# Attention's score tiles: 4 tokens by 16 heads, two stacked on the partitions, in place of 8 tokens by 16 heads

## What is computed

```python
qkv = qkv.reshape(n, t, 3, H, DH)                 # H = 16, DH = 18
q, k, v = (qkv[:, :, 0], qkv[:, :, 1], qkv[:, :, 2])
attn = jnp.einsum('nthd,ntkd->nthk', q * scale, k)  # 16 x 16 for each token
attn = jax.nn.softmax(attn, axis=-1)
out = jnp.einsum('nthk,ntkd->nthd', attn, v)
```

## Time and profile before

| | |
|---|---|
| median of 3 runs | 426.82 us (426.48 to 428.12) |
| the profiled execution | 426.86 us |
| its span, first instruction to last | 425.1 us |
| PE busy | 402.0 us (95%) |
| PEld busy | 262.3 us (62%) |
| DVE busy | 290.0 us (68%) |
| ACT busy | 232.0 us (55%) |
| granted TensorE clock | full (1.0) in every stretch |

### The profile page before, as it was taken

The page is one execution under the profiler, slowest core; times in us unless marked ns, Lnnn a source line. Parts: engine busy times, 40 slices in busy tenths (PEclk is TensorE's granted clock), DMA queues, the critical chain, the costliest instruction groups (busy, mean ns, idle before and its releaser), DMA issues.

```text
span 425.1 us, 11334 instructions
## 1 busy us (share of the span) xinstructions
PE 402.0 (95%) x4579; PEld 262.3 (62%) x4579; DVE 290.0 (68%) x792; ACT 232.0 (55%) x485; POOL 112.6 (26%) x133
## 2 busy tenths in 40 slices
PE   8999999999989999999977888879999999999996
PEld 4665555666556666666645565657755566666675
DVE  2688885677678846667667866666989776646452
ACT  3356434432266988987786686565776351422100
POOL 5039999950009600000000000004520110101040
PEclk9999999999999999999999999999999999999999
DMA  5999000000000000000000000000000000000011
GB/s 163 303 316 269 24 4 3 11 8 0 2 0 2 2 2 3 2 3 3 2 4 3 5 3 5 2 3 2 2 0 2 14 29 14 15 28 15 29 43 42
DMA packets 7926, 14.68 MB, mean 35 GB/s; under 512 B 2555, under 2 KB 6239, under 8 KB 7748
## 3 DMA queue, kind: packets, MB, share of 16 engines
q1 hardware_dynamic: 7874, 13.96, 11.0%
HBM read 11.52 MB, written 2.38 MB: 33 GB/s over the span
## 4 chain that ended last, share of the span: by engine, by line
PE 74%; DVE 12%; ACT 9%; issue 5%; ACTq 0%; DVEq 0%
PE psum L943 13%; PE psum L959 12%; PE psum L509 9%; PE psum L789 7%; PE psum L773 3%; DVE MX L1356 2%; ACT scratch L1054 2%; PE psum L609 2%; PE psum L866 2%; PE psum L691 2%; PE psum L920 2%; PE psum L621 2%; ACT big L1087 2%; PE psum L737 2%; PE psum L714 2%
## 5 line engine op out<-in xcount | busy, mean ns | idle before, releaser
L943 PE MATMUL psum<-scratch,W 128*128 128x512 f16 (+1 forms) x252 | 57.9, 379 | 0.0
L959 PE MATMUL psum<-W,big 128*128 128x288 f16 x432 | 55.1, 286 | 0.0
L498 POOL TENSOR_TENSOR X<-X,big 128x288 f32<-128x288 f32 x16 | 13.0, 825 | 152.8 <-ACT big L1160 152.5
L1185 ACT ACTIVATE big<-psum 128x512 f32<-128x512 f32 x36 | 21.3, 597 | 57.3 <-PE psum L943 52.3
L959 PEld LDWEIGHTS psum<-W,big 128*128 128x128 f16 x432 | 42.2, 98 | 12.9
L789 PE MATMUL psum<-WQ,scratch 128*128 128x288 f16 (+1 forms) x336 | 49.2, 287 | 1.1 <-DVE scratch L1351 1.1
L1356 DVE TENSOR_REDUCE MX<-psum 128x8 f32<-128x1024 f32 x32 | 39.0, 1220 | 10.9 <-PE psum L737 10.5
L509 PE MATMUL psum<-ident 128*32 128x192 f32 (+3 forms) x142 | 42.7, 385 | 0.0
L1115 ACT ACTIVATE big<-psum 128x1024 f32<-128x1024 f32 x32 | 32.9, 1032 | 14.2 <-PE psum L829 13.9
L943 PEld LDWEIGHTS psum<-scratch,W 128*128 128x128 f16 (+1 forms) x252 | 24.7, 98 | 25.6
L1054 ACT ACTIVATE scratch<-psum,MOD 128x512 f32<-128x512 f32 (+3 forms) x48 | 34.3, 772 | 10.3 <-PE psum L714 6.2
(11 more groups left out here) (218 smaller groups left out, 781.2 us busy)
## 6 DMA issues: line engine op xcount, KB each, us to landing
X<-in_x_dram SPq DMA_DIRECT2D x4, 576.0 KB, 15.1
out_dram<-big SPq DMA_DIRECT2D x16, 144.0 KB, 1.7
big<-in_L_cond_W_dram SPq DMA_DIRECT2D x1, 2268.0 KB
big<-in_L_cond_ada_w_dram SPq DMA_DIRECT2D x2, 864.0 KB, 18.4
stage<-in_L_cond_fc_w_dram SPq DMA_DIRECT2D x1, 1296.0 KB, 19.0
big<-in_L_cond_fc_w_dram SPq DMA_DIRECT2D x1, 1152.0 KB
stage<-in_L_cond_qkv_w_dram SPq DMA_DIRECT2D x1, 864.0 KB
big<-in_L_cond_fc_w_dram SPq DMA_DIRECT2D x3, 144.0 KB
```

The source lines that it names most:

```text
L943: mm = pe.matmul(FB[idx % 3], W1[0:r, w_, P * m:P * m + P], HT[0:r, n % 2, a_, :], start=(p_ == 0), stop=(p_ == 6))
L959: mm = pe.matmul(YB[t % 2][:, 0:D], g[:, a_, f, cols], W2[:, w_, f, :], start=(f == 0 and a_ + w_ == 0), stop=(f == NF - 1 and w_ == 1))
L1185: act.activation(G32[:, idx % 2, :], FB[idx % 3], ACT.Gelu, scale=1.0 / (FINE * FINE)).then_inc(gelu_sb, 1)
```

## The change

A score tile now has 4 tokens x 16 heads = 64 rows and 64 columns, and two such tiles (`e` = 0, 1) stand one above the other on the partitions of the same columns. A unit still fills 128 x 1024 of PSUM, but its 32 tiles hold 128 tokens. So there are 16 units, exponentials and maxima in place of 32, a group is 2 units in place of 4, and AHEAD holds 8 maxima, one in each three slots. The matmuls of a unit are more and smaller. All values_out are ACT's, and v_late's four parts stand in one step. The core of the diff:

```diff
+        pairs = sb("pairs", [P, P])
-        OT = [scratch[:, o + a_ * 5 * CH // 2:o + a_ * 5 * CH // 2 + CH] for a_ in range(2)]
+        OT = scratch[:, o:o + 2 * CH].rearrange("p (a e j) -> p a e j", a=8, e=2)
-        UNITS = 16 * B
+        UNITS = 8 * B
+        HALF = P // 2
-        AHEAD = {24 + 3 * s_ // 2: s_ for s_ in range(16)}
-        LATER = {st: 1 for st in range(16)}
-        ROWS_LATER, ROWS_BANK = {8: 2, 16: 3}, {8: VB[0], 16: MXB[0]}
-        PAIRED = 18
-        DVE_AT = 17
+        AHEAD = {24 + 3 * s_: s_ for s_ in range(8)}
+        LATER = {st: 1 for st in range(8)}
+        ROWS_LATER, ROWS_BANK = {4: 2, 8: 3}, {4: VB[0], 8: MXB[0]}
+        PAIRED = 8
@@ pool: a permutation for the turn after the loop, in place of ident @@
+            for e in range(2):
+                chain(pool.tensor_copy(pairs.rearrange("p (h e m) -> p e h m", h=H, e=2)[:, e],
+                                       ident[:, P // 2 * e:P // 2 * e + P // 2].rearrange("p (h m) -> p h m", h=H)))
@@ maxima (scores has the same loops, with MROWS + 1 rows) @@
-                for g in range(4):
-                    for c_ in range(2):
-                        mm = pe.matmul(MXB[c_][:, P * g:P * g + P], operand(s_, c_, 0, g, MROWS), operand(s_, c_, 1, g, MROWS),
-                                       start=True, stop=True)
+                for g in range(8):
+                    for e in range(2):
+                        for c_ in range(2):
+                            mm = pe.matmul(MXB[c_][HALF * e:HALF * e + HALF, HALF * g:HALF * g + HALF], operand(s_, c_, 0, g, e, MROWS),
+                                           operand(s_, c_, 1, g, e, MROWS), start=True, stop=True)
@@ values @@
-                for c_ in range(2):
-                    if q == 0 and w:
-                        pe.wait_ge(ot_ready, 2 * w + c_ - 1)
-                    for g in range(4):
-                        mm = pe.matmul(PO[c_][32 * g:32 * g + 32, P * q:P * q + P], VG[:, w % 2, c_, 4 * q + g, :],
-                                       E[:, s_ % 2, c_, P * g:P * g + P], start=True, stop=True)
+                    if w:
+                        pe.wait_ge(ot_ready, 2 * w)
+                for q in (2 * q2, 2 * q2 + 1):
+                    for c_ in range(2):
+                        for g in range(4):
+                            for e in range(2):
+                                rows, at, to = slice(HALF * e, HALF * e + HALF), HALF * (4 * (q % 2) + g), HALF * (4 * c_ + q)
+                                mm = pe.matmul(PO[e][32 * g:32 * g + 32, to:to + HALF], VG[rows, w % 2, c_, 4 * q + g, :],
+                                               E[rows, s_ % 2, c_, at:at + HALF], start=True, stop=True)
@@ the loop of PE @@
-                if st % 4 < 2 and 4 <= st // 4 + 1 < UNITS // 4:
-                    for q in range(2 * (st % 4), 2 * (st % 4) + 2):
-                        v_late(st // 4 + 1, q)
-                if st >= 4 and st % 4 == 2:
-                    turn_values(st // 4 - 1)
-                if st % 4 == 3 and st // 4 + 1 < UNITS // 4:
-                    v_groups(st // 4 + 1)
+                if st % 2 == 0 and 4 <= st // 2 + 1 < UNITS // 2:
+                    for q in range(4):
+                        v_late(st // 2 + 1, q)
+                if st >= 2 and st % 2 == 1:
+                    turn_values(st // 2 - 1)
+                if st % 2 == 1 and st // 2 + 1 < UNITS // 2:
+                    v_groups(st // 2 + 1)
@@ the loop of ACT @@
-                if st < DVE_AT:
-                    if st >= 4 and st % 4 == 0:
-                        values_out(st // 4 - 1)
+                if st >= 2 and st % 2 == 0:
+                    values_out(st // 2 - 1)
```

More of the change, by code:

```diff
@@ L826, in scores @@
                     pe.wait_ge(mr_ready, 2)
-                for g in range(4):
-                    for c_ in range(2):
-                        mm = pe.matmul(SB[s_ % 2 if s_ > PAIRED else 0][c_][:, P * g:P * g + P], operand(s_, c_, 1, g, MROWS + 1),
-                                       operand(s_, c_, 0, g, MROWS + 1), start=True, stop=True)
+                for g in range(8):
+                    for e in range(2):
+                        for c_ in range(2):
+                            mm = pe.matmul(SB[s_ % 2 if s_ > PAIRED else 0][c_][HALF * e:HALF * e + HALF, HALF * g:HALF * g + HALF],
+                                           operand(s_, c_, 1, g, e, MROWS + 1), operand(s_, c_, 0, g, e, MROWS + 1),
+                                           start=True, stop=True)
                 mm.then_inc(s_ready, 1)
@@ L1127, in values_out @@
             def values_out(w):
-                act.wait_ge(pv_ready, 4 * w + 4)
+                act.wait_ge(pv_ready, 2 * w + 2)
                 if w >= 1:
                     act.wait_ge(o_turned, 2 * w)
-                for c_ in range(2):
-                    act.copy(OT[c_], PO[c_]).then_inc(ot_ready, 1)
+                for e in range(2):
+                    act.copy(OT[:, :, e, :], PO[e].rearrange("p (a j) -> p a j", a=8)).then_inc(ot_ready, 1)
             def v_late_out(w, q):
@@ L1146, in _ @@
                     act.mul(MRT[:, ROWS_LATER[st], :], ROWS_BANK[st][0:64, 0:P], 1.0 / MROW).then_inc(mr_ready, 1)
[L1147 to L1154 removed]
+                if st >= 2 and st % 2 == 0:
+                    values_out(st // 2 - 1)
+                    if st // 2 + 1 == 4:
+                        for q in range(4):
+                            v_late_out(st // 2 + 1, q)
+                if st % 2 == 1 and st // 2 + 1 < UNITS // 2:
+                    v_out(st // 2 + 1)
             def product_out(t):
@@ L1449, in normalise @@
                                       ALU.mult).then_inc(o_norm, 1)
-            def values_out(w):
-                dve.wait_ge(pv_ready, 4 * w + 4)
-                dve.wait_ge(o_turned, 2 * w)
-                for c_ in range(2):
-                    dve.tensor_copy(OT[c_], PO[c_]).then_inc(ot_ready, 1)
             def v_late_out(w, q):
@@ L1464, in _ @@
                     maximum(s_)
-                if st >= DVE_AT and st % 4 == 0:
-                    values_out(st // 4 - 1)
-                if st % 4 < 2 and 4 < st // 4 + 1 < UNITS // 4:
-                    for q in range(2 * (st % 4), 2 * (st % 4) + 2):
-                        v_late_out(st // 4 + 1, q)
-                if st >= 4 and st % 4 == 2:
-                    normalise(st // 4 - 1)
+                if st % 2 == 0 and 4 < st // 2 + 1 < UNITS // 2:
+                    for q in range(4):
+                        v_late_out(st // 2 + 1, q)
+                if st >= 2 and st % 2 == 1:
+                    normalise(st // 2 - 1)
             dve.wait_ge(o_norm, UNITS // 2)
```

66 lines of the change are left out of this document (31 added, 35 removed).

## The result

The changed kernel takes 435.0 us (median) against 426.7: slower by 1.9%, ratio 1.0188, interval 1.0160 to 1.0217. The prediction was 412.6. The loop of the first reads much the same (74.2 us in place of 73.0). Against the 425.1 us before, the 432.4 are 7.3 longer: QKV stage - 3.4, attention loop + 10.8, the rest - 0.1. The loop, from the first exponential to the last turn's start, was forecast to go from 62.2 to 51.4; it went to 73.0, as far the other way.

What follows compares the result with a forecast made beforehand. No engine was full in the loop; a ring of waits once per 256-token group set the pace. 426.9 less 3.4 (QKV stage) and 10.8 (loop) gave 412.7, forecast as 412.6 us; 405 to 421 held about 8 in 10.

Steps and rivals of the forecast that it cites:

- The QKV stage: Second half of the QKV stage: eight fewer maxima and three fewer waits, less 0.5 for ACT's couplings, gain 3.4 us.
- The waits of maxima for DVE: QKV stage: three waits, 1.3 us, go because maxima no longer stand in neighbouring slots.
- A burst of maxima: Maxima or scores unit: 32 matmuls on four quarters running together move the next burst by 0.33 us, as before.
- dearer bursts: Rival, QKV stage and loop: quarters run two at a time, scores + 0.24 and values + 0.40 a group; 419.4 us, chance 0.17.
- Values: Values burst in the loop: 64 f32 records on eight tiles take 0.65 us, moving the next by 0.57.
- The copies for `pairs`: Two small copies on POOL before PE first needs its constants: well under 1 us, covered, costed at nothing.
- the shorter runs in the copies: ACT's and DVE's copies: runs of 4 elements instead of 8, costed at nothing; a tenth in QKV would be 1 us.
- The table load: End of the loop: ACT's 1.28 us table load comes behind the last copies and stays hidden by 0.3 us.
- The ring itself: Attention loop: chain of waits from one group's first exponential to the next's, 6.1 us against 7.9; groups 4 to 6, 6.8.
- The first step that failed: Burst sizing: L852's 32 matmuls move the next burst by 0.40 us, so the number of matmuls alone costs no more.
- start rate: Rival, QKV stage and loop: TensorE can't start matmuls fast enough, p ns a record; 432 us at p = 25, chance 0.10.
- the clock's rival: Rival, loop: PE's clock falls to 1.2 GHz, doubling 2.4 us of ring matmuls in 7 groups; 430 us, chance 0.04.

Runs made afterwards that it cites:

- the first: Changed kernel's first run, median 435.0 us; a disturbance made its profiled rotation 13 us longer, so the profile shown is a second run's.
- Run 2: Kernel before, with each matmul of maxima, scores and values made as two of 64 moving columns; 888 more matmuls in the loop cost 5.0 us.
- Run 8: Kernel before with a 16-bit values product, one record for each matmul of values in place of two; loop 3.3 us longer.
- Runs 1: Changed kernel again, unchanged, for an undisturbed profile; span 432.4 us, loop 73.0 us.
- 13: Changed kernel with 32 small 16-bit matmuls (64 instructions) added behind the first scores; loop 2.5 us shorter.
- 14: Changed kernel with 64 small 16-bit matmuls (128 instructions) added behind the first scores; loop 13.5 us longer.
- 5: Changed kernel with 16 f32 fillers of 8 columns (64 instructions) behind the first scores; the fillers themselves take 3.9 us.
- 6: Changed kernel with 32 f32 fillers of 8 columns (128 instructions) behind the first scores; loop 22.2 us longer, the fillers themselves 12.3.
- 15: Changed kernel with 96 small 16-bit matmuls (192 instructions) added behind the first scores; loop 85.9 us.
- run 12: Changed kernel with the 16-bit values product and fillers of 320 columns in the loop to keep TensorE busy; 419.9 us.
- run 7: Changed kernel with a 16-bit values product, one record for each matmul of values in place of two; 422.9 us.
- run 17: Kernel before with 64 small matmuls (128 instructions) added behind its first scores; one stall of 1.90 us, first group 10.4 us in place of 7.8.
- 3: Changed kernel with 12 fillers of 320 columns in the loop to keep TensorE busy; loop 1.4 us shorter.
- 9: Changed kernel with the 16-bit values product, and v_groups and v_out moved one step later, behind values; 421.7 us.
- 10: Changed kernel with 16-bit values, v_groups and v_out one step later, and late V columns through the maxima's banks; 419.2 us.

## Why the prediction was wrong

**What held.** The QKV stage: 3.4 us forecast, 3.4 measured from the start of the span and 3.2 from the stage's first product (it began 0.3 earlier). The waits of maxima for DVE are gone. A burst of maxima moves what follows by 0.38 at full clock, as a burst of scores does (forecast 0.33): four quarters do run together, and dearer bursts, the rival at 419, did not come in this size. Values were undersized: 0.85 us in place of 0.65, moving the next by 0.78 in place of 0.57. Its 0.65 was taken over from four tiles to eight with no row that had eight. The copies for `pairs` and the shorter runs in the copies cost nothing that shows. The table load is 1.28 us and ends before ACT is wanted, with 0.23 us to spare (0.3 forecast).

**The ring itself** nearly held, where nothing disturbed it. A late group at full clock without a stall:

```profile
268.07 1.03 ACT L1126 ACTIVATE big<-psum 128x1024 f32<-128x1024 f32 x1
...
270.74 0.45 PE L836 MATMUL psum<-big 63*64 63x64 f16 x32
271.22 0.85 PE L877 MATMUL psum<-big,scratch 64*32 64x64 f32 x64
272.00 1.09 PE L893 MATMUL psum<-ident,scratch 128*128 128x128 f32 x8
274.25 0.56 PE L860 MATMUL psum<-SELV,big 36*128 36x18 f16 x32 [1.16 <-DVE stage L1456]
...
275.44 1.03 ACT L1126 ACTIVATE big<-psum 128x1024 f32<-128x1024 f32 x1
```

That is 7.37 us where 6.8 was forecast. The turn starts 3.93 after the exponential and not 3.4, by the longer values and by scores that queue behind the late columns; from the turn to the next exponential it is 3.44, forecast 3.41. Eight such errors are 2 to 4 us. By this estimate they would have left the kernel at 415 to 417.

**The first step that failed** stands under the size of the bursts: "L852's 32 matmuls of 18 columns move the next burst by 0.40 us, so the number alone does not cost more". True of one burst at a time. I summed the bursts as if the next one could always begin. A group of 256 tokens has 96 more records than before (128 more in the first four groups, with their maxima) and was to take 6.1 us in place of 7.9; nothing in the sum asked where the instructions come from, and the runs show 8.5 us of waits in the loop, all at place 193 or 194 of a block. The rival that came nearest, start rate, had the wrong mechanism: it priced each record at p ns. (Its 1,088 records are 1,024 by the profile, so that p = 25 gives 431 and not 432.) Run 2 shows 5.6 ns, in lumps of up to 0.8 us. Yet its 25 ns come back as the pace of the supply: 296 records are 592 instructions with their weight loads, or 2.3 fetches; in 6.1 us these would lie 2.6 us apart, and no trace has two less than 3.25 apart. That pace makes some 7.5 us of a group, an estimate. The late group of 7.37 us above, without a stall, thus ran at the edge of it: its blocks' places 194 were reached 2.7 us after the fetch began. The trace of before had the numbers for the right mechanism: its fetches of 256 instructions, each 0.9 to 1.5 us long. The Trainium skill, in "Advanced Engine Details and Errata", section "ISA Cache", says that an engine's instructions are cached in lines of 16 KB, 256 instructions, and that there are only two such lines. The traces agree with the 256. How many lines there are no run here tells. The prediction did not weigh it; by it, bursts of more than the instructions left would have had to be looked for.

**The second** is the weight of the clock's rival, 0.04. It rested on 64% of busy time "still granted in full", and on a share of 61% that left v_late out. Here the 3.4 us before the fall at 220.6 were as busy. The second row is a stretch of the kernel before:

```profile
217.20:220.60 3.40, 2.18 (x164) 1.80 (x160) 1.22 (x1) 3.21 (x6) 0.00 (x0) 1.00 0.02 5
```

```profile
280.50:283.90 3.40, 1.95 (x44) 1.26 (x40) 2.20 (x5) 2.51 (x3) 0.00 (x0) 1.00 0.00 0
```

2.18 of 3.40 us is 64%, and then the clock was at half for 20 us. The kernel before was busy for 1.95 of 3.40, 57%, and kept it in full. So PE's busy share alone did not tell when the clock falls, and was no ground for so small a weight. The page's row of the granted clock (slices of 10.8 us) shows how long in all:

```profile
PEclk9999999999999999999975857989999999999999
```

Run 8 shows that it falls with shorter bursts alone, without a stall. The clock's price on the ring came out near the estimate, in part by luck: group 4, at half clock over most of it and with one stall of 1.54 us on the way, took 11.2 where its like at full clock took 7.4. Of the 3.8 more, the stall is 1.5 and max_turn's copy 0.3; 2.0 are left, and the prediction had said 2.4 a group. But it had the ring's matmuls double, and not all do: from full to half clock values moves the next by 1.11 in place of 0.79 us, the turn lasts 1.97 in place of 1.09, and v_groups 0.60 in place of 0.56. That is 1.2; the rest of the 2.0 lies off the terms that it named.

**How the 21.6 us between 51.4 and 73.0 split** I can only estimate. Runs 1, 13 and 14 are one program, shifted. With their fillers' time taken off, three equations (base, a price for each us of "issue", one for each us at half clock) give 53.7 us, 0.60 and 0.35: 5 us for the stalls and 14 for the clock. A fit through all seven runs of that program (the first profile and 5, 6, 15 too) gives some 54.8, 0.95 and 0.20: 8 and 8, with errors up to 2 us. Both put the undisturbed loop at 54 to 55 us, 2 to 4 above the forecast, so the time would be 415 to 417 us, and the disturbances at 16 to 19. How much belongs to each stays open, since the two rise together over these runs, and other kernels don't bear the clock's price out: run 8 is 3.3 us longer for 37.5 us at half clock, 0.09 each, and run 12 has 41 us less of it than run 7 and a loop shorter by 0.7. They may also feed each other: the clock fell 2.1 us after a stall ended in run 1 (at 247.9) and 2.3 after one in run 17 (at 226.7).

**So the change** did what it says to ACT and DVE, and the ring, where undisturbed, was shortened nearly as forecast. All of it was given back by TensorE, which was not the bound: its matmuls became too many and too short for the supply of instructions, which runs 2, 13 to 15 and 17 show, and its clock fell. Why the clock falls where it does is not shown.

## What to carry to other kernels

When a change halves the size of matmuls, count instructions too. In these traces the changed kernel, with a fetch every 4 us, stalled, and the kernel before, with one every 4.7 to 7.7, did not. Bursts decide: what counts is whether the 40 to 140 instructions that are left when a fetch begins last for the 2.5 us until it can be used. If the label "issue" appears inside a burst, number the instructions of that queue. This kernel's loop moved by 13 us with 64 matmuls of 0.7 us put ahead of it, so two versions whose programs differ in length are not compared by their time alone. And on a ring of waits, an edit that leaves TensorE less to do needs its clock priced with it: the kernel before got 0.6% slower from a cheaper product.

## What the runs showed of the hardware

- TensorE stalled for up to 2.5 us at instruction 193 to 195 of a block of 256, whatever stood there (L743, L836, L860, L877, L893, L756 and others; 100 stalls of over 0.45 us in 18 traces), and went on 2.15 to 2.95 us after the last fetch had begun. Fetches took 0.9 to 1.5 us and never began less than 3.25 us apart.
- Matmuls start far closer than 25 ns apart, the least that the Trainium skill gives in "TensorE: Matmul & The Clock Gate", section "Wait — 56ns, not 53.3ns?": 64 over four quarters take 0.73 us, 11 ns each (run 14's first row above). The measurement decides for a burst over four quarters. Over 256 instructions the fetches' least distance, 3.25 us, is again 25 ns a matmul.
- Records of 8 columns in f32 with weights of 128 columns start 0.11 us apart at full clock and 0.21 at half (run 6's fillers), although they move only 8 columns.
- A clock still at half at the loop's last turn lengthens what follows by 1.4 us (143.0 in place of 141.6, runs 3, 7, 9 and 10).
- Granted clock: full again at 241.1 us, at half again at 247.9, after the 1.61 us stall and the wait behind it had left PE busy for 3.1 of 6.8 us:

```profile
241.10:247.90 6.80, 3.12 (x179) 2.38 (x177) 2.27 (x4) 3.28 (x7) 0.00 (x0) 1.00 0.01 2
```
